# A graph-transformer layer: root rows between the aggregation's passes, gather slots in other tiles, and edge weights summed panel by panel

## What is computed

```python
def _rgcn_conv(x, src, dst, etype, W, root, b):
    x_src = x[src]
    seg = dst * num_rel + etype
    sums = jax.ops.segment_sum(x_src, seg, num_segments=num_nodes * num_rel)
    cnt = jax.ops.segment_sum(jnp.ones((src.shape[0],), dtype=x.dtype), seg, num_segments=num_nodes * num_rel)
    mean = sums / jnp.maximum(cnt, 1.0)[:, None]
    mean = mean.reshape(num_nodes, num_rel, -1)
    out = jnp.einsum('nri,rio->no', mean, W)
    return out + x @ root + b
...
xn = _layernorm(x, axis=-1)
h = jax.nn.relu(_rgcn_conv(xn, ..., W1, root1, b1))
gnn = _rgcn_conv(h, ..., W2, root2, b2)
x = x + gnn + mix(xn)
x = x + ffn(_layernorm(x, axis=-1))
```

## Time and profile before

| | us |
|---|---|
| median of 3 runs (3419.77 to 3424.31) | 3421.99 |
| the profiled execution | 3421.39 |
| its span | 3419.5 |
| PE busy | 3174.5 (93%) |
| DVE busy | 1773.6 (52%) |
| POOL busy | 1273.2 (37%) |
| ACT busy | 762.8 (22%) |

### The profile page before, as it was taken

How to read it: one execution, slowest core, us unless ns; L and a number is a source line. 1 busy time by engine, 2 the same in 40 slices (tenths; PEclk the granted TensorE clock), 3 DMA queues, 4 the chain that set the end, 5 groups by cost and what they waited for, 6 DMA issues and landing times.

```text
span 3419.5 us, 64810 instructions
## 1 busy us (share of the span) xinstructions
PE 3174.5 (93%) x19556; PEld 2359.9 (69%) x19557; DVE 1773.6 (52%) x2941; ACT 762.8 (22%) x1086; POOL 1273.2 (37%) x1377
## 2 busy tenths in 40 slices
PE   6999999999997999999899989999886999999999
PEld 5788888777776888888677766776654555555555
DVE  7576666555555333333555552334586456455551
ACT  2211121000001212211000004444212543543540
POOL 2681000577772000002777761000420632652562
PEclk9999999999999999999999999999998999999999
DMA  5334334599994232321898882000330000000003
GB/s 149 101 106 149 118 116 137 171 306 307 306 306 140 87 120 94 118 95 63 319 307 307 303 287 78 14 28 14 88 95 24 20 1 19 19 1 19 19 28 95
DMA packets 101141, 433.58 MB, mean 127 GB/s; under 512 B 19648, under 2 KB 19971, under 8 KB 96818
## 3 DMA queue, kind: packets, MB, share of 16 engines
q0 software_dynamic: 55712, 266.87, 23.2%
q1 hardware_dynamic: 42593, 124.83, 11.6%
q10 hardware_dynamic: 2736, 40.50, 3.4%
HBM read 355.21 MB, written 76.88 MB: 126 GB/s over the span
## 4 chain that ended last, share of the span: by engine, by line
PE 71%; DVE 12%; issue 7%; DVEq 6%; ACT 1%; POOL 1%; DMA 1%; POOLq 0%; SPq 0%; ACTq 0%
PE PS L1466 26%; PE PS L1580 13%; PE PS L1776 5%; PE PS L1604 3%; PE PS L1711 3%; PE PS L1475 3%; DVE NM L1387 2%; PE PS L1612 2%; PE PS L1759 2%; PE PS L1760 2%; PE PS L1715 2%; PE PS L1649 2%; DVE HOT L1166 2%; PE PS L1633 2%; PE PS L1623 1%
## 5 line engine op out<-in xcount | busy, mean ns | idle before, releaser
L1466 PE MATMUL PS<-WHL,XT 128*125 (+1 forms) x3240 | 549.4, 329 | 7.0 <-DVE WHL L940 4.2
L1466 PE MATMUL PS<-WHL,HT 128*125 (+1 forms) x3240 | 531.8, 327 | 0.0
L1580 PE MATMUL PS<-GATA,HOT 128*125 128x384 f16 x2880 | 492.6, 328 | 37.0 <-issue 17.8
L1466 PEld LDWEIGHTS PS<-WHL,XT 128*125 (+1 forms) x3240 | 441.3, 138 | 92.7 <-issue 5.3
L1466 PEld LDWEIGHTS PS<-WHL,HT 128*125 (+1 forms) x3240 | 441.9, 137 | 84.2
L558 POOL DMA_INDIRECT GATA<-msg_table,SKEY x432 | 421.8, 976 | 163.0 <-issue 124.6
L1580 PEld LDWEIGHTS PS<-GATA,HOT 128*125 x2880 | 386.3, 137 | 114.5 <-issue 44.6
L1166 DVE SCALAR_TENSOR_TENSOR HOT<-NODE,DSTF,WHLO x720 | 297.0, 475 | 277.6 <-issue 277.6
L594 POOL TENSOR_TENSOR PL<-PF 125x500 bf16<-125x500 f32 (+1 forms) x360 | 320.6, 924 | 281.0 <-ACT PF L797 277.8
L1016 DVE SCALAR_TENSOR_TENSOR MSG<-PS,MSG 125x768 f16<-125x768 f32 x160 | 153.1, 957 | 360.3 <-ACT MSG L627 358.9
L627 ACT ACTIVATE MSG<-PS 125x768 f16<-125x768 f32 x160 | 129.6, 810 | 786.8 <-PE PS L1466 773.9
(11 more groups left out here) (254 smaller groups left out, 3898.6 us busy)
## 6 DMA issues: line engine op xcount, KB each, us to landing
msg_table<-MSG SPq DMA_DIRECT2D x160, 336.0 KB
WST<-in_wg_dram ACTq DMA_DIRECT2D x16, 2304.0 KB, 10.1
WST<-in_wf_dram SPq DMA_DIRECT2D x7, 1536.0 KB, 6.3
KROW<-key_rows POOLq DMA_DIRECT2D x54, 192.0 KB, 3.8
GATA<-msg_table,SKEY POOLq DMA_INDIRECT x432, 4.5
msg_table<-MSG SPq DMA_DIRECT2D x160, 39.0 KB
WST<-in_wm_dram SPq DMA_DIRECT2D x5, 1152.0 KB, 5.1
...
```

Source lines behind the costliest of these rows:

```text
L1466: ins = pe.matmul(PS[0:ROWS, b0 + h, 0:HALF], X[:, xp, k, bass.ts(t, ROWS)], panel_part(slot, wp, k, h), start=k == 0 and xp + wp == 0, st ...
L1580: ins = pe.matmul(PS[0:ROWS, bass.ds(((n + (L + 1)) % 2) * 2 + h, 1), 0:HALF].rearrange("p a c -> p (a c)"), HOT[:, bass.ds((n % 2) * AT + ...
```

## The change

- **Root rows.** A table ROOT_AT names which root rows PE makes between groups. Layer 1: rows 0 to 4 ahead, row 5 just ahead of the first pass, rows 6 to 9 ahead of groups 15, 30, 45 and 60. Layer 2: rows 0 to 2 ahead, row 3 just ahead of the first pass, rows 4 to 9 ahead of groups 9, 21, 33, 45, 57 and 69. They use banks 4 and 5, each waits until the row before it is taken, and DVE takes one behind two more groups. What DVE does behind a root row (scales, split_low) goes with it. The loop of passes becomes a function that stands in the program once per piece.
- **Bias.** ACT copies it into ROOT during the last relation panel (root_made), and DVE's take reads ROOT.
- **Slots.** GATB 4, ROW 4 (seen as fp16), MSG 2, GATC 2; HOT has its own place. Layer 2's wait for the last root row is gone.
- **Edge weights.** POOL adds each relation's part when that panel's weight is known (relation_in); at relations_made one multiplication is left. In layer 1 the rest (inverse count, split) comes behind the first twelve gathers.
- **Release.** DVE, not PE, counts group_used, behind the last take that it makes in a group's turn of its loop; POOL waits for one count more. The 1x1 matmul is gone.
- **Drain.** In DVE's loop it moves from ahead of the HOTs to between them and the take.
- **WPR.** Its load waits for the end of layer 2's aggregation.

```diff
+ROOT_AT = (((0, 5), (5, 6), (10, 7), (15, 8), (20, 9)), ((0, 3), (3, 4), (7, 5), (11, 6), (15, 7), (19, 8), (23, 9)))
...
-            return GATB[:, k, :] if k < AT else GATA[:, k - AT, :]
+            return GATB[:, k, :] if k < AT else GATR[:, k - AT, :] if k < 2 * AT else MSG[:, k - 2 * AT, :] if k < 2 * AT + 2 else GATC[:, k - 2 * AT - 2, :]
...
             sp.dma_start(RF[:].rearrange("p a m -> p (a m)"), a["rf"]).then_inc(S["rf_in"], 16)
-            sp.wait_ge(S["bias_free"], 3)
-            sp.dma_start(WPR[:], a["wmp"]).then_inc(S["wp_in"], 16)
...
-            sp.wait_ge(S["group_used"], 2 * AG)
+            sp.wait_ge(S["group_used"], 2 * (AG + 1))
+            sp.dma_start(WPR[:], a["wmp"]).then_inc(S["wp_in"], 16)
...
+            def relation_weight(L, r):
+
+                g.wait_ge(S["relation_in"], L * REL + r + 1)
+                g.sem_inc(S["pool_tick"], 1)
+                if r == 0:
+                    g.tensor_scalar(WSUM[:], ETF[:, 0:TILES], 0.0, GW[:, 0:1], ALU.is_equal, ALU.mult)
+                else:
+                    g.tensor_scalar(TMPF[:], ETF[:, 0:TILES], float(r), GW[:, r:r + 1], ALU.is_equal, ALU.mult)
+                    g.drain()
+                    g.tensor_tensor(WSUM[:], WSUM[:], TMPF[:], ALU.add)
+                g.drain()
...
             for L in range(2):
-                edge_weights(L)
+                if L == 1:
+                    for r in range(REL):
+                        relation_weight(1, r)
+                common_weight(L)
+                if L == 1:
+                    edge_weights(1)
                 g.wait_ge(S["msg_out"], ROW_IN * REL * RT * (L + 1))
                 g.sem_inc(S["pool_tick"], 1)
                 for t in range(TILES):
                     grp, k = t // AT, t % GSLOTS
+                    if L == 0 and t == GSLOTS:
+                        edge_weights(0)
                     if t % AT == 0:
                         if grp >= GSETS:
-                            g.wait_ge(S["group_used"], AG * L + grp - GSETS + 1)
+                            g.wait_ge(S["group_used"], (AG + 1) * L + grp - GSETS + 2)
                             g.sem_inc(S["pool_tick"], 1)
                         elif L == 1:
-                            g.wait_ge(S["group_used"], AG)
+                            g.wait_ge(S["group_used"], AG + 1)
                             g.sem_inc(S["pool_tick"], 1)
-                            if grp == 1:
-                                g.wait_ge(S["acc_done"], 2 * ROW_SUMS + 1)
-                                g.sem_inc(S["pool_tick"], 1)
...
+                def root_row(t, b0):
+
+                    v.drain()
+                    v.wait_ge(S["root_made"], RT * L + t + 1)
                     v.wait_ge(S["acc_done"], t + (ROW_SUMS * L + REL * RT + 2))
-                    v.scalar_tensor_tensor(halves(ROOT[:, t, :]), rowps(2 * (t % 2)), OUTINV[:], halves(BIAS[:]), ALU.mult, ALU.add).then_inc(S["pair_out"], 1)
+                    v.scalar_tensor_tensor(halves(ROOT[:, t, :]), rowps(b0), OUTINV[:], halves(ROOT[:, t, :]), ALU.mult, ALU.add).then_inc(S["pair_out"], 1)
...
+                for t in range(ROOT_AT[L][0][1]):
+                    root_row(t, 2 * (t % 2))
 
                 def take_pass(n):
 
+                    v.drain()
                     v.wait_ge(S["pass_done"], n + (L + 2))
...
+                def passes(first, end):
+
+                    with v.Fori(first, end) as grp:
+                        lo, hi = group_blocks(v, grp)
+                        with v.Fori(lo, hi) as b:
+                            n = v.snap(cnt, min_val=0, max_val=1 << 20)
+                            v.wait_ge(S["pass_done"], n + (L + 1))
+                            for k in range(AT):
...
+                            take_pass(n)
+                            v.reg_mov(was, b)
+                            v.reg_add(cnt, cnt, 1)
+                        v.sem_inc(S["group_used"], 1)
+
+                v.wait_ge(S["root_made"], RT * (L + 1))
+                first = 0
+                for i, t in ROOT_AT[L]:
+                    passes(first, i * GSETS + 2)
+                    root_row(t, 4)
+                    first = i * GSETS + 2
+                passes(first, AG)
...
-                        pe.matmul(PS[0:1, 6, 0:1], ZERO[:, 0:1], ZERO[:, 0:1], start=True, stop=True).then_inc(S["group_used"], 1)
+                def root_row(t):
+
+                    pe.wait_ge(S["pair_out"], REL * RT + t + (ROW_SUMS * L + 2))
+                    row_products(X, t, (REL + L) % 2, 4, S["acc_done"])
+                    weights_top(t)
...
+                for n_, (i, t) in enumerate(ROOT_AT[L]):
+                    root_row(t)
...
+                    passes(i, ROOT_AT[L][n_ + 1][0] if n_ + 1 < len(ROOT_AT[L]) else AG // GSETS)
```

More of the change, by code:

```diff
@@ L116, in graph_and_attentions_kernel @@
         FILL = sb(qctx, "FILL", [128, KT * D - 6 * 128 - N], f32)
-        ROW = sb(top, "ROW", [ROWS, 4, D], f32)
+        ROWS4 = sb(top, "ROW", [128, 4, D], f32)
+        ROW = ROWS4[0:ROWS]
+        GATR = ROWS4[:].bitcast(f16)
         IDF = sb(top, "IDF", [128, 128], f32)
@@ L1557, in _, with weights_top @@
                     panel(p, RT // 2 if L == 0 else 0)
-                panel(REL, TAIL // 2 if L == 0 else 0)
+                pe.wait_ge(S["w_lo"], (REL + 1) * (L + 1))
+                def weights_top(t):
+                    if t == 3:
+                        top_transpose((REL + 1) * (L + 1))
+                    elif t == 5:
+                        top_broadcast((REL + 1) * (L + 1))
+                for t in range(ROOT_AT[L][0][1]):
+                    row(REL, t, t % 2)
+                    if L == 0 and t < TAIL:
+                        find_counts(REL * RT + t - COUNTED * RT)
+                    weights_top(t)
@@ new lines, in _ @@
+                for n_, (i, t) in enumerate(ROOT_AT[L]):
+                    root_row(t)
+                    if n_ == 0:
+                        q0 = pe.snap(cnt, min_val=0, max_val=1 << 20) + L
+                        pe.wait_ge(S["pass_out"], q0 + 1)
+                        for h in range(2):
+                            ins = pe.matmul(PS[0:ROWS, bass.ds((q0 % 2) * 2 + h, 1), 0:HALF].rearrange("p a c -> p (a c)"), ZERO[:, 0:ROWS], ZERO[:], start=True, stop=True)
+                        ins.then_inc(S["pass_done"], 1)
+                    passes(i, ROOT_AT[L][n_ + 1][0] if n_ + 1 < len(ROOT_AT[L]) else AG // GSETS)
```

136 lines of the change are left out of this document (60 added, 76 removed).

## The result

The changed kernel takes 3428.98 us (median of 20 runs, 3426.06 to 3432.64), the kernel before 3420.14 us in the same comparison: a ratio of 1.0026, 95% interval 1.0020 to 1.0033, some 9 us slower. The profiled execution has a span of 3428.2 us against 3419.5. The forecast was +9.8 us.

A forecast was written before the change was run, and what follows sets the result against it. The gatherer's 5.13 us a group bounded the kernel before; VectorE's cycle would set the new pace. Layer 1 at +7.1 and layer 2 at +2.7 us gave +9.8 on 3421.39, 3432 us as a median, range 3400 to 3460.

The forecast's parts named there:

- The sum: All terms of both aggregations added: layer 1 +7.1 us, layer 2 +2.7 us, together +9.8 us; work behind each unchanged.
- VectorE's cycle: VectorE's HOT-to-HOT step per group in the aggregation: 4.78 us, bounds 4.35 and 4.9, counted 81 times a layer.
- First HOTs: Start of aggregation on VectorE: 621.6 in layer 1, 1587.8 in layer 2; first take's wait adds 0.7 and 1.9 us.
- Crossings: Groups straddling two blocks of nodes need a second pass: 3.3 us each, nine a layer, 29.7 us.
- late release: Slots released by VectorE's take behind the next group's HOTs, about one pass later: costed at nothing.
- The cover that I named: Gatherer's spare time against late slots: 2 x 4.78 us against 8.4 us of issue and landing, 1.2 us between.
- Moved rows: Root rows made between groups, four in layer 1, six in layer 2: 6.0 us each, bounds 3.5 and 7.1.
- loop entries: Leaving and entering the pass loop for each moved row: 0.4 us each, 1.6 us in layer 1, 2.4 in layer 2.
- The split: VectorE's split of the next weight panel, now alone between two passes: +4.1 us in layer 1, +1.7 in layer 2.
- Rival A: The moved drain in VectorE's loop is free, cycle stays at TensorE's 4.35 us: 3405 us, chance 0.22.
- Rival B: The gatherer stays the aggregation's bound and the rows vanish in its reserve: 3348 us, chance 0.08.
- Rival C: Loop copies need code fetched at jumps back: cycle 4.90 us, each entry 1.3 us, 3460 us, chance 0.18.

The follow-up runs named there:

- experiment 2: The changed kernel with TensorE's 1x1 matmul, not VectorE, releasing a group's slots: 3404.76 us, ratio 0.9955 to the kernel before.
- experiment 6: As experiment 2, but VectorE still counts up a semaphore that nobody waits for, once per group: 3417.64 us, ratio 0.9991 to the kernel before.
- Experiment 3: The changed kernel with all root rows made ahead of the passes, none between groups: 3439.19 us, ratio 1.0059 to the kernel before.
- experiment 5: The changed kernel with TensorE releasing the slots and the drain back ahead of the HOTs: 3400.22 us, ratio 0.9942 to the kernel before.
- experiment 1: The changed kernel with VectorE's drain back ahead of the HOTs: 3417.67 us, ratio 0.9992 to the kernel before.
- experiment 8: The changed kernel with 24 more drains on VectorE ahead of layer 1's first pass, shifting the loop copies: 3423.86 us, ratio 1.0009 to the kernel before.

## Why the prediction was right, point by point

- **The sum** said +9.8 us; measured +8.7 in the span, +8.8 between the medians. Layer 1: +7.1 forecast, +5.5 measured once the 2.45 us ahead of it are taken out. Layer 2: +2.7 forecast, +2.5 measured (it begins 4.6 us late and ends 7.1 us late). Another 1.6 us arise in the first rows of layer 2's panels and 1.6 behind the second aggregation; I had put both at nothing. The first goes with the clock: from 1060 to 1110 the mean granted clock is 0.83 of full speed, 0.86 before, which is 1.5 us in 50; what lowered it was not tested, and for the second no run shows a cause. The two together are about what the early start of this one execution gave back, so the agreement of the sum is better than it deserves by some 2 us.
- **VectorE's cycle** of 4.78 us was the term that carried the sum. Measured between the first HOTs of two groups: 4.67 to 4.68 (medians) in four long pieces of layer 1 and 4.84 in the fifth (mean 4.70), 4.75 in five pieces of layer 2 and 5.01 and 5.03 in two (mean 4.84). The take-to-HOT interval of the earlier trace rows and a drain-and-dispatch of 0.42 to 0.49 us were the right rows. Its make-up was not quite mine: 0.11 us of it is the new semaphore instruction, which I did not name.
- **First HOTs**: 619.75 for 621.6, 0.6 us late once the 2.45 us ahead are taken out; layer 2's at 1590.82, 1.6 us earlier than forecast on its own clock, but the first take then waited 4.04 us for row 3 and the cleared bank, for which I had 1.9:

```profile
1590.82 1.65 DVE L1193 SCALAR_TENSOR_TENSOR HOT<-NODE,DSTF,WHLO  x4 [1.24 <-issue]
1596.50 1.02 DVE L1178 SCALAR_TENSOR_TENSOR ROOT<-PS,GS,ROOT  x1 [4.04 <-PE PS L1645]
```

- **Crossings, the mis-sized step.** I put 3.3 us on each and nothing on the late release. The time was right all the same. The second pass of a group costs 3.0 us on VectorE as said (3.1), but the step behind it is 5.97 us instead of 4.70 in layer 1: 4.3 us a crossing. With TensorE's release that step is 5.45 at a plain step of 4.59 (experiment 2), and 5.46 at the change's own plain step (experiment 6). In layer 2 it is 5.69, and 5.32 in experiment 6. The cover that I named, 1.2 us, was gone after most crossings (two of layer 1's eight steps, 4.99 and 5.00 us, show no loss): of the 11.3 us in all (experiment 6 against the change) some 8 stand in the steps behind crossings. The failed step is "I cost it at nothing".
- **Moved rows, mis-sized the other way.** I took 6.0 us each. Steps that hold a row are 8.8 and 9.1 us in layer 1 (rows 8 and 9), 9.1 to 9.8 in layer 2, against 4.70 and 4.75: 4.1 to 5.0 us. Two rows stand apart: layer 1's row 6 falls behind a crossing and costs 5.9, and layer 2's row 5 with its scales has a step of 11.5. Experiment 3 gives about the same from outside: ten rows win 10.2 us of 59, so they cost 4.9 each with all that hangs on them (crossings too: the step behind one is 6.6 and 6.5 us in experiment 3). Both layers together, the crossings cost some 15 us more than forecast and the rows with their loop entries some 16 less. These errors nearly cancel, and that is luck: it is why the sum was better than its parts.
- **The split** cost 4.1 us by forecast; the step with row 7 is 13.7 us against 8.8 and 9.1, 4.7 more. In the trace of the changed kernel it stands alone as said:

```profile
791.94 1.02 DVE L1178 SCALAR_TENSOR_TENSOR ROOT<-PS,GS,ROOT  x1 [4.96 <-PE PS L1632]
793.13 1.02 DVE L1155 SCALAR_TENSOR_TENSOR ROOT<-PS,OUTINV,ROOT 125x768 f32<-125x768 f32 x1 [0.18 <-issue]
794.07 5.01 DVE L864 SCALAR_TENSOR_TENSOR WHL<-WST,SC,WHL 128x4608 f16<-128x4608 f32 x1
798.99 1.64 DVE L1193 SCALAR_TENSOR_TENSOR HOT<-NODE,DSTF,WHLO  x4
```

  In layer 2 the forecast was 1.7; the step with row 7 is 9.8 us, no longer than rows 6 and 8 (9.6 and 9.7): nothing, though in experiment 5 it is 12.6 against 10.8.
- **Rival A** (the drain is free) rested on the rule of the Trainium skill, "VectorE: DVE Perf Modes", section "The DRAIN you can't avoid". The forecast left out what the same paragraph adds, that a next operation which is not held starts earlier; the take at 732.42 in experiment 1, ahead of the HOTs' end, agrees with that. Experiment 1 speaks against a free drain: 11.3 us for its place. The traces show 0.42 us of idle ahead of the take that is not there with the drain in its old place. I read it as the sequencer, which may not queue the take behind the drain; no run tells this from another cause inside the engine. The rival's price was off as well: with the drain back the time is 3417.67 us, above its 3392 to 3413, since the semaphore instruction and the late slots stay.
- **Rival B** fell with the waits: the gatherer is no bound of the change. It waits for VectorE for longer than the 30 us a layer that I named: behind the thirteenth gather 38 us in layer 1 and 47 in layer 2.
- **Rival C** was right in kind and too dear. The Trainium skill's "Runtime: NRT & Kernel Launch", section "Instruction fetch mechanics", lets a branch cost a fetch by where its target lies; three of fourteen copies were slow by 0.17 to 0.28 us, and experiment 8 changed which ones by moving the code. The two instruction packets in the 17 steps of a slow piece speak against a fetch at each branch. Leaving and entering the loop cost little: HOT stands 1.12 to 2.24 us behind a root row's work, where every step has 1.6 us.
